# Routing made in nine units inside the edge gather, and one fetch for a token and its marks

## The reference

```
x = x + gnn(layernorm(x), ...)            # out[dst] += norm * (mems[src] @ W), top-7 neighbours of r
h = layernorm(x)
logits = h @ gate_w + gate_b
probs = softmax(logits);  idx = argmax(probs);  prb = probs[idx]
one_hot = one_hot(idx, 8)
pos = (cumsum(one_hot, axis=0) * one_hot).sum(-1) - 1     # place of a token in its expert
kept = pos < 1954
ybuf = relu(buf @ w1[e] + b1[e]) @ w2[e] + b2[e]          # buf: the kept tokens, by expert and place
x = x + ybuf[idx, pos] * prb * kept
```

## Time and profile before

| | |
|---|---|
| median of 3 runs | 2775.74 us (2775.42 to 2777.63) |
| the profiled execution | 2778.93 us, its span 2777.4 us |
| busy in the span | PE 1957.6, PEld 1693.0, DVE 1365.4, ACT 564.4, POOL 1724.7 us |
| POOL, edge gather (L638) | 1214.3 us busy in 1248 issues |
| POOL, experts (L686, L688, L699) | 124.7, 123.2, 130.2 us in 128 issues each |
| time from the last group add to the first expert fetch | 1891.85 to 1981.62 us |

### The profile page before, as it was taken

How to read it: one execution, slowest core, us unless ns; L and a number is a source line. 1 busy time by engine, 2 the same in 40 slices (tenths; PEclk the granted TensorE clock), 3 DMA queues, 4 the chain that set the end, 5 groups by cost and what they waited for, 6 DMA issues and landing times. The chain is left out here.

```text
span 2777.4 us, 37613 instructions
## 1 busy us (share of the span) xinstructions
PE 1957.6 (70%) x11154; PEld 1693.0 (61%) x11155; DVE 1365.4 (49%) x3695; ACT 564.4 (20%) x1066; POOL 1724.7 (62%) x1774
## 2 busy tenths in 40 slices
PE   2002777776677677667777798884798799799964
PEld 1002555765566566556666788883687688688753
DVE  6999787235523641552432355545543345344322
ACT  0047100210021012002112132321132223222221
POOL 6741477777777777777777777770245544534455
PEclk7556888998899889989989899996899899899987
DMA  9116233663366346446556677774012212212211
GB/s 266 49 38 178 80 99 102 202 191 103 103 195 198 103 141 208 146 118 208 169 150 208 205 214 215 219 202 131 18 38 71 68 37 68 69 36 69 66 36 30
DMA packets 231936, 350.51 MB, mean 126 GB/s; under 512 B 38888, under 2 KB 165128, under 8 KB 231620
## 3 DMA queue, kind: packets, MB, share of 16 engines
q0 software_dynamic: 79808, 198.30, 25.1%
q1 hardware_dynamic: 151796, 149.91, 18.4%
q10 hardware_dynamic: 144, 0.20, 0.0%
HBM read 296.73 MB, written 56.40 MB: 127 GB/s over the span
## 5 line engine op out<-in xcount | busy, mean ns | idle before, releaser
L638 POOL DMA_INDIRECT arena<-z_table,arena x1248 | 1214.3, 973 | 484.1 <-issue 368.8
L1617 PE MATMUL bank<-arena 128*128 128x128 f32 x4992 | 746.7, 312 | 383.1 <-DMA arena<-z_table,arena 193.7
L1617 PEld LDWEIGHTS bank<-arena 128*128 128x128 f32 x4992 | 691.7, 222 | 482.2 <-issue 395.8
L1183 DVE TENSOR_TENSOR nodes<-nodes,bank 128x256 f32 x312 | 131.5, 421 | 854.6 <-PE bank L1617 849.1
L1843 PE MATMUL bank<-arena 128*128 128x256 f32 (+1 forms) x1472 | 331.6, 385 | 25.6 <-issue 18.6
L699 POOL DMA_INDIRECT out<-arena x128 | 130.2, 1017 | 317.7 <-DVE arena L1502 305.8
L1855 PE MATMUL bank<-arena 128*128 128x256 f32 (+1 forms) x1472 | 326.1, 380 | 0.0
L1843 PEld LDWEIGHTS bank<-arena 128*128 128x128 f32 x1472 | 284.2, 197 | 66.6 <-issue 28.1
L758 ACT ACTIVATE arena<-arena 128x512 f32<-128x512 uint16 (+1 forms) x125 | 135.4, 1086 | 810.0 <-DVE arena L1202 460.7
L1855 PEld LDWEIGHTS bank<-arena 128*128 128x128 f32 (+1 forms) x1472 | 273.1, 188 | 39.8 <-issue 1.0
L849 ACT ACTIVATE arena<-bank,arena 128x256 f32<-128x256 f32 (+1 forms) x368 | 151.9, 465 | 415.8 <-PE bank L1843 415.8
(11 more groups left out here) (306 smaller groups left out, 1848.7 us busy)
## 6 DMA issues: line engine op xcount, KB each, us to landing
arena<-z_table SPq DMA_DIRECT2D x120, 512.0 KB
arena<-z_table,arena POOLq DMA_INDIRECT x1248
arena<-in_L_ffn_w SPq DMA_DIRECT2D x16, 1024.0 KB
z_table<-nodes SPq DMA_DIRECT2D x14, 896.0 KB, 6.7
x_rows<-nodes SPq DMA_DIRECT2D x98, 128.0 KB
arena<-in_x SPq DMA_DIRECT2D x48, 256.0 KB, 4.0
out<-nodes SPq DMA_DIRECT2D x96, 128.0 KB
nodes<-in_x SPq DMA_DIRECT2D x12, 896.0 KB, 11.5
```

Source lines behind the costliest of these rows:

```text
L638: nc.gpsimd.indirect_dma_start(gath[:, slot, t, :], None, z_table, bass.IndirectOffsetOnAxis(ap=src_idx[:, tile_at:tile_at + 1], axis=0)). ...
L1183: nc.vector.tensor_tensor(where, where, agg_bank[step % AB][:, 0:D].rearrange("p (k c) -> p k c", k=KD), ALU.add).then_inc(S["agg_added"], 1)
L1617: last = nc.tensor.matmul(agg_bank[i][:, k * P:(k + 1) * P], gath[:, i, t, k * P:(k + 1) * P], sel[:, i, t, :], start=(t == 0), stop=(t == ...
```

## The change

**Units.** The batches are joined into nine units: seven of two batches (12 windows), one of one batch (6) and the last of two (8). `full(u)` is the step in which the last logits of the unit are made: 258, 266, ..., 306, then 310 and 320. It is of kind C. In the words of the unit's steps, counted from `full(u)` = step 0, DVE takes each pair's logits (L1320), makes the maximum and the difference in step 0 (`gate_unit`), ACT the exponential in step 1 (`exp_unit`), DVE softmax, choice and a running count in step 1 (`choose_unit`, 10 to 13 instructions), PE two rank matmuls in step 2 ahead of the group's sum (`rank_unit`), DVE place, gate mark and one-hot parts in step 2 (`place_unit`, 12 instructions), and DVE `list_block` for two windows each, two blocks in each of steps 3, 4 and 5; PE takes these blocks at the head of steps 4, 5 and 6 (`list_rows`). The carry between units is the last column of the running count.

**Banks.** Logits, ranks and totals go to free columns of the group's own bank `agg_bank`, so PE makes the logits ahead of the group's sum and no longer behind it. The list has bank 5.

**Marks.** `m_rows` is gone. `x_rows` has rows of 260 words, the four marks behind the 256 features. The Newton step writes `rstd` and shift into `marks`, from which ACT reads them; SP stores the marks of a unit in nine DMAs of 16 bytes per token. `fetch` issues one indirect DMA per 128 rows, where there were two.

**The rest.** The first expert's weights are loaded by ACT at step 312 and the second's by SP behind the last group, ahead of the routing's end; `b1` is loaded and transposed ahead of the node batches. The batch loop of PE has eight steps in its body and four turns, with the steps around it unrolled. The branch for unsorted groups has its own copy of the old routing; it isn't taken.

```diff
+    UNIT_BATCHES = [(b, b + 1) for b in range(0, NB - 3, 2)] + [(NB - 3,), (NB - 2, NB - 1)]
+    def full(u):
+        b = UNIT_BATCHES[u][-1]
+        return begin(b) + 2 * PAIRS_IN[b] + 4
+    def units_at(step, after):
+        return [u for u in range(NUN) if full(u) + after == step]
+    def blocks_at(step, after):
+        return [BLOCK0[u] + i for u in range(NUN) for i in range(BLOCK0[u + 1] - BLOCK0[u])
+                if full(u) + after + i // 2 == step]
...
                 for t in range(2):
                     rows = list_i[:, 2 * n + t:2 * n + t + 1]
-                    nc.gpsimd.indirect_dma_start(xs_rows[:, slot, t, 0:D], None, x_rows,
-                                                 bass.IndirectOffsetOnAxis(ap=rows, axis=0)).then_inc(S[f"xs_in{slot}"], 16)
-                    nc.gpsimd.indirect_dma_start(xs_rows[:, slot, t, D:XW], None, m_rows,
+                    nc.gpsimd.indirect_dma_start(xs_rows[:, slot, t, :], None, x_rows,
                                                  bass.IndirectOffsetOnAxis(ap=rows, axis=0)).then_inc(S[f"xs_in{slot}"], 16)
...
+            def choose_unit(u):
...
+                dve.wait_ge(S["gate_out"], u + 1)
+                then(nc.vector.tensor_reduce(norm[:, w0:w1], gates, AX.X, ALU.add))
+                then(nc.vector.reciprocal(norm[:, w0:w1], norm[:, w0:w1]))
+                then(nc.vector.tensor_tensor(gates, gates, over(norm[:, w0:w1], w), ALU.mult))
+                then(nc.vector.tensor_reduce(best[:, w0:w1], gates, AX.X, ALU.max))
...
+                nc.vector.tensor_tensor_scan(flat[0], flat[1], flat[2], 0.0, ALU.mult, ALU.add).then_inc(S["pick_ok"], 1)
...
+            def list_block(n):
...
+                nc.vector.tensor_tensor(list_lo[:, n % 2, :, :], iota_r[:, :].unsqueeze(1).to_broadcast([P, LW, P]),
+                                        pos_lo[:, w:w + LW].unsqueeze(2).to_broadcast([P, LW, P]), ALU.is_equal).then_inc(S["list_in"], 1)
...
             def node_work(step):
...
-                for b in takes_of(step):
-                    take_batch(b)
+                for n in blocks_at(step, 3):
+                    list_block(n)
+                for u in units_at(step, 2):
+                    place_unit(u, step)
+                for u in units_at(step, 1):
+                    choose_unit(u)
+                for b, j in logits_of(step):
+                    take_logits(b, j, step)
+                for u in units_at(step, 0):
+                    gate_unit(u)
...
+            def node_step(step, r):
+                for n in blocks_at(step, 4):
+                    list_rows(n, r)
...
+                for b, j in logits_of(step):
+                    logit_pair(b, j, step, r)
+                for u in units_at(step, 2):
+                    rank_unit(u, step, r)
+                if step < NG:
+                    add_up(step % BODY)
```

More of the change, by code:

```diff
@@ new lines, in _ @@
+                turn(nc.vector.tensor_copy(marks[:, :, RSTD - D], rstd2[:, :]))
+                turn(nc.vector.tensor_copy(marks[:, :, SHIFT - D], shift2[:, :]))
+                dve.wait_ge(S["rep_list"], 1)
+                HW = NW // 2
+                for i in range(2):
+                    rows = slice(i * HW, (i + 1) * HW)
+                    turn(nc.vector.tensor_copy(gate_t[:, rows, :], bank[2 + i][:, 0:HW * NE].rearrange("p (w e) -> p w e", e=NE)))
+                for e in range(NE):
+                    turn(nc.vector.tensor_tensor_scan(gate_l[:, :, e], ones[:, 0:NW], gate_t[:, :, e], 0.0, ALU.mult, ALU.add))
@@ new lines, in _ @@
+                turn(nc.vector.tensor_copy(taken_f[0:1, :], gate_l[0:1, NW - 1, :]))
+                turn(nc.vector.tensor_copy(taken_i[0:1, 0:NE], taken_f[0:1, :]))
+                turn(nc.vector.tensor_tensor(gate_l, gate_l, gate_t, ALU.subtract))
+                for i in range(2):
+                    rows = slice(i * HW, (i + 1) * HW)
+                    turn(nc.vector.tensor_tensor(gate_l[:, rows, :], gate_l[:, rows, :],
+                                                 bank[i][:, 0:HW * NE].rearrange("p (w e) -> p w e", e=NE), ALU.add))
@@ L1726, in logit_pair, with rank_unit @@
                 last.then_inc(S["logit_ps"], 1)
-            def node_step(step):
+            def rank_unit(u, step, r):
+                to = agg_bank[step % AB]
+                pe.wait_ge(S["pick_ok"], r + (u + 1))
+                flat = [t[:, :, :].rearrange("p e w -> p (e w)") for t in (pick_cum, pick_u)]
+                nc.tensor.matmul(to[:, RANK:TOTAL], ones[:, :], flat[0], start=True, stop=False)
+                last = nc.tensor.matmul(to[:, RANK:TOTAL], tri_less, flat[1], start=False, stop=True)
+                if u == NUN - 1:
+                    last = nc.tensor.matmul(to[:, TOTAL:TOTAL + NE], ones[:, :], pick_cum[:, :, UW], start=True, stop=True)
+                last.then_inc(S["rank_ps"], 1)
@@ new lines, in list_rows @@
+            def list_rows(n, r):
+                pe.wait_ge(S["list_in"], r * (2 * R_BLOCKS) + 2 * (n + 1))
+                for i in range(LW):
+                    last = nc.tensor.matmul(list_bank[:, 0:NE * CT], list_lo[:, n % 2, i, :],
+                                            list_hi[:, n % 2, i, :, :].rearrange("p e t -> p (e t)"),
+                                            start=(n == 0 and i == 0), stop=(n == NLB - 1 and i == LW - 1))
+                last.then_inc(S["list_ps"], 1)
@@ L1729, in node_step @@
                 for b, j in convs_of(step):
[L1730 to L1732 removed]
+                    convolve(b, j, r)
                 for b, j in turns_of(step):
[L1734 to L1736 removed]
@@ L1757, in _ @@
-            for q in range(15, 17):
-                for i in range(BODY):
-                    group(i, q, s0, before)
-                    node_step(s0 + BODY * q + i)
-            for step in range(NG, END):
-                node_step(step)
+                    turn_pair(b, j, r)
+            pe.wait_ge(S["w_conv"], 4 * 16)
+            nc.tensor.transpose(turn_bank[:, 0:NE * FT], b1_rows[0:NE * FT, :], ident[0:NE * FT, 0:NE * FT]).then_inc(S["b1_ps"], 1)
+            LOOP0, LOOPS = G2 + 6 * BODY, 4
@@ L1765, in _ @@
+            for step in range(G2, LOOP0):
+                node_step(step, 0)
+            with pe.Fori(0, LOOPS) as r:
+                for step in range(LOOP0, LOOP0 + R_STEPS):
+                    node_step(step, r)
+            for step in range(LOOP0 + LOOPS * R_STEPS, END):
+                node_step(step, 0)
             n_bad = pe.value_load(bad_i[0:1, 0:1], min_val=0, max_val=GROUPS)
```

440 lines of the change are left out of this document (262 added, 178 removed).

## The result

The changed kernel takes 2790.11 us (median of 5 runs, 2788.94 to 2791.73) against 2775.74 us: 1.0043 times the kernel before, 95% interval 1.0032 to 1.0054. The forecast was 2795. The profiled execution has a span of 2790.2 us, before 2777.4.

What follows compares the result with a forecast made beforehand. POOL's issuing of fetches was taken to set the gather's pace. 2778.9 profiled - 49.3 (tail) - 20 (experts) + 89 (gather) = 2798.6, forecast as 2795 us since the profiled execution is 3.2 over the median; range 2738 to 2838.

Steps and rivals of the forecast that it cites:

- The sign and its mechanism: Whole kernel: 0.7% slower, as PE and DVE waiting for each other in the gather cost more than tail and experts gain.
- Per unit: Gather with node batches: eight steps take 53.8 us, 49.6 at full clock plus 4.2 for PE's slow clock.
- turn at full clock: Gather: the intervals between group adds of a unit's eight steps sum to 49.6 us without clock loss.
- The clock's 29 us: Gather: sums behind PE's waits in steps 2 and 4 run slow, 1.7 and 2.5 us a unit, some 29 in all.
- rival 2: Gather: round trips run at full clock, so the loss is 60 us in place of 89, total 2766; chance 0.20.
- Rival 3: Gather: the clock stays low over steps 4 to 6, 5.6 us more per unit, total 2834; chance 0.12.
- The prediction's reading of the earlier trace: PE's clock: after a wait of 2.81 us a sum took 3.77 us, after one of 1.30 it took 2.05.
- Steps 307 to 311: Gather's end: taken as a full unit's first four intervals, 33.9 us in place of 24.9.
- Tail: Last group add to first expert fetch: 40.5 us against 89.8, so 49.3 us less, ends 43 and 55.
- Experts: First fetch to end: half the fetch issues go, saving 20 us where POOL has the chain, ends 15 and 26.
- Rival 1: Gather: the ring's slots hide the round trips, POOL keeps the pace, 4 us lost in all, total 2710; chance 0.13.
- The rule on small writes: Marks' stores in the gather: 16-byte pieces, 1536 a unit, would take more of the DMA engines than their bytes, yet fit.

Runs made afterwards that it cites:

- PE kept busy: Changed kernel with dummy matmuls on PE ahead of two waits per unit, 8 before the rank, 26 before the first list rows: 2770.12 us, 0.9976 of the kernel before.
- The undone fetch: Changed kernel with marks in their own table again and two indirect fetches per 128 rows: 2808.09 us, 1.0114 of the kernel before.
- the fetch alone: Kernel before with only the marks stored behind the rows and one fetch per 128 rows, routing still behind the gather: 2757.67 us, 0.994 of the kernel before.
- `list_behind_sum`: Changed kernel with PE's list rows issued behind the step's group sum instead of ahead of it: 2731.57 us, 0.9833 of the kernel before.
- `both_loosened`: Changed kernel with list rows behind the group sum, and rank, places and blocks one step later: 2723.3 us, 0.9802 of the kernel before.
- `both_blocks_spread`: Changed kernel with list rows behind the sum, rank and places a step later, and one block a step over six steps: 2710.55 us, 0.9763 of the kernel before.

## Why the prediction came out right

By its own steps:

- **The sign and its mechanism** held: the round trips cost more than the shorter tail and the halved fetches give. With the same work, the order on PE alone moves the kernel from 2790 to 2732 us, and the same blocks spread over more steps move it to 2847.
- **Per unit**: 53.8 forecast, 54.25 in the typical one. Interval by interval, steps 1 to 6: 10.21 (forecast 8.15 + 1.7), 7.65 (7.6), 10.26 (7.25 + 2.5), 6.55 (6.65), 7.46 (7.45), and 12.12 for the rest (12.5). The turn at full clock, forecast 49.6, is 49.9 with PE kept busy.
- **The clock's 29 us**: 4.5 us a unit where PE was kept busy, forecast 4.2; rival 2 (full clock) is out by that, and by the turn of 54.6. Rival 3 (low over steps 4 to 6) is out as a rule, since most sums of steps 5 and 6 took 2.0 us, but it has a part: in two of the six turns the sum of step 6 was slow, which the forecast had at nothing. The prediction's reading of the earlier trace rows, that the length of a wait decides the clock, is too simple: in the kernel before, too, a sum behind 1.56 us of idle PE took 3.55 us (at 1720.13) and one behind 1.85 us took 2.05 (at 1754.84).
- **Steps 307 to 311**: a term that failed. Forecast 33.9 us, measured 23.35. I took them as a full unit's first four intervals, but the selection of four steps ahead has ended there, and the last two batches begin a turn late, so DVE and PE have less to do. Against these 10.5 us too much, the six turns took 4.6 more than forecast (the two slow sums are 3.3 of it), and step 259 was already 3.0 us late, for which the forecast had no term. That the gather's loss came out at 85.6 for 89 is thus in part luck.
- **Tail** 43.0 for 40.5: 26.8 us to the last logits (forecast 26.1), 16.2 from there (14.4). The excess of that part is mostly PE at its low clock (0.50 from 2014.3 to 2018.3): DVE waits 0.70 us for a block's slot and 1.44 for the last block.
- **Experts**: -26.0 for -20. Waits shortened by 4.6, 2.0 and 4.3 (forecast 5.0, 2.5, 5.0), first rows by 1.2 (1.9), and the stretch from the third of these waits to the end by 8.3 in place of 5.0. A pause of 5.52 in PE's second stage became 2.98, which I had not counted. The undone fetch takes back 22.2 of the 26, and the fetch alone gives 20.9; the other 4 us are not accounted for by a run. They may be no effect at all: with one fetch and the same code of the experts, this stretch took between 769.4 and 774.8 us in the changed kernel and the eight built from it with that fetch, and the changed kernel's 769.8 is near the low end. The mechanism held; a gain of 21 to 26 stands against the 20.
- **Rival 1** (slots hide the round trips, 2710) described no run of the changed kernel, but it does describe the kernel once PE's waits are moved behind the sums: its turn of 41 us and its 2710 stand beside 41.6 and 2710.55 of the fastest one. The agreement to a microsecond is luck: the parts differ by up to 5 us from the rival's, and the profiled execution of that kernel took 2717.5.
- **The rule on small writes** from the Trainium skill ("DMA: Bandwidth & Descriptors", "Specifications"), by which pieces under 512 bytes don't reach the full rate and are read, modified and written: the row above gives 0.32 x 85 x 16 / 12,560 = 0.035 us of an engine for 16 bytes, and 0.198 x 85 x 16 / 4342 = 0.062 us for a packet of 1.4 KB on q1. So a piece costs far more than its bytes, in line with the page, though no row shows how it is written. By an estimate from this row, 1536 of them a unit are 54 us shared by 16 engines, 3.4 us of the DMA's time in 54; PE's waits for gathered rows are 1.2 us in the whole stretch, and undoing the stores moved the last add by 5.6 us at most.

## What to carry to other kernels

Work moved under a running pipeline costs not its busy time but the waits it puts between two engines that did not wait for each other before: look for each operand of the in-order engine that is made behind its previous output, and issue its consumer behind the next output, or a step later if nothing heavy stands ahead of its maker there. Count a matmul engine's long waits twice: once for the idle time, and once for the slow clock of what may follow. When a change has separable parts, time each alone: here one part was a gain by itself, and the other became one by an order of instructions.

## What the runs showed of the hardware

- Behind 2.41 us of idle PE the next sum of 16 matmuls took 3.55 us, and behind 0.18 us 2.03, with the same work between; dummy matmuls that add zeros filled that wait. The length of the wait alone doesn't settle it: behind 1.22 us the sum took 2.03 us in four turns and 3.34 and 3.66 in two of the changed kernel, and behind 2.82 us, with the list rows and a convolution between, 1.95 in `list_behind_sum`.
- An indirect fetch takes POOL 0.95 us; beside four DVE operations of 128x256 elements in a row, eight of the 25 that overlapped such operations took 2.0 to 2.2 us in `both_loosened`. With one block a step (`both_blocks_spread`) none did, though five took 1.5 to 1.6. What the two engines share was not tried. The Trainium skill, "SBUF — State Buffer", section "SBUF: two separate sides", says that POOL can't write a fetch's descriptors while DVE runs an operation in a two-port mode, and that a DVE operation with two SBUF inputs shuts out a POOL operation that reads SBUF. The block operations have two inputs each; the rows agree in direction, with about 1.2 us more for such a fetch, but no run here shows that either is the cause.
- A 16-byte store behind each row, 12,544 in one DMA, took about 0.035 us of a DMA engine per piece, and 27 us of 16 engines' time in all; under the building of the list it added nothing (last add to first fetch 89.7 us, before 89.8).
